# A fused cross-attention, attention and feed-forward layer: the engines' hand-written orders are rewritten

## What is computed

```python
x = x + matmul(fake_quant(layernorm(x)), fake_quant(ctx))   # ctx: [16, 1024, 1024], a matrix per sequence
q, k, v = split(layernorm(x) @ Wqkv)                        # 32 heads of 32, one k and one v head
probs = softmax(where(causal, q @ k.T * scale + alibi, -1e30))
x = x + (probs @ v) @ Wo
r = softmax(layernorm(x) @ gate_w.T)                        # 8 experts
x = x + (layernorm(x) * (r @ in_scale)) @ sign(weight).T * (r @ out_scale) + bias
```

## Time and profile before

| | |
|---|---|
| median of 3 runs | 466.38 us (464.2 to 466.59) |
| profiled execution, its own time | 469.97 us |
| its span in the profile | 468.1 us |
| busy: PE, DVE, ACT, POOL | 383.6, 314.0, 262.5, 127.6 us |
| moved by transfers | 91.96 MB |
| mean granted clock of TensorE | 0.905 |

### The profile page before, as it was taken

How to read it: one execution, slowest core, us unless ns; L and a number is a source line. 1 busy time by engine, 2 the same in 40 slices (tenths; PEclk the granted TensorE clock), 3 DMA queues, 4 the chain that set the end, 5 groups by cost and what they waited for, 6 DMA issues and landing times.

```text
span 468.1 us, 9132 instructions
## 1 busy us (share of the span) xinstructions
PE 383.6 (82%) x3712; PEld 253.2 (54%) x3712; DVE 314.0 (67%) x591; ACT 262.5 (56%) x309; POOL 127.6 (27%) x144
## 2 busy tenths in 40 slices
PE   0447825699795979989998999899989999989877
PEld 0116713594352577548754784478446945865354
DVE  7578576759747328874887489657975696486342
ACT  4787874565566855846484648473847372234021
POOL 4210041003610202603171317131623052116031
PEclk9956986599897979989998999899989999999958
DMA  8999985596748991659256846773675000100001
GB/s 322 378 410 409 406 326 179 191 406 208 254 148 295 260 355 46 228 224 282 99 194 259 209 145 214 270 213 126 225 270 158 3 1 1 47 1 1 0 22 70
DMA packets 30384, 91.96 MB, mean 196 GB/s; under 512 B 8256, under 2 KB 8512, under 8 KB 30336
## 3 DMA queue, kind: packets, MB, share of 16 engines
q1 hardware_dynamic: 28464, 84.45, 50.9%
q10 hardware_dynamic: 1872, 6.82, 4.2%
HBM read 85.50 MB, written 4.19 MB: 192 GB/s over the span
## 4 chain that ended last, share of the span: by engine, by line
PE 45%; DVE 24%; ACT 11%; DMA 6%; issue 6%; SPq 3%; POOL 3%; ACTq 0%; DVEq 0%
PE R L1558 9%; DMA ring<-ctx 6%; ACT b L573 6%; PE T L1386 4%; DVE st L926 3%; PE T L1509 3%; PE R L1422 3%; PE T L1467 3%; PE R L1425 3%; PE R L1424 3%; DVE XS_lo L876 3%; PE C L1367 3%; PE R L1338 2%; PE R L1339 2%; PE R L1340 2%
## 5 line engine op out<-in xcount | busy, mean ns | idle before, releaser
L573 ACT ACTIVATE b<-ring,quant,qpar 128x2048 uint8<-128x2048 f32 x64 | 132.5, 2091 | 15.0 <-DMA ring<-ctx 7.5
L1422 PE MATMUL R<-T_hi,Wqkv_hi 128*128 128x128 f16 x448 | 80.7, 224 | 0.0
L1424 PE MATMUL R<-T_lo,Wqkv_hi 128*128 128x128 f16 x448 | 80.5, 223 | 0.0
L1425 PE MATMUL R<-T_hi,Wqkv_lo 128*128 128x128 f16 x448 | 80.4, 223 | 0.0
L1367 PE MATMUL C<-b,aT 128*64 128x512 f16 x256 | 38.2, 435 | 21.6 <-ACT b L573 20.0
L329 POOL TENSOR_TENSOR Pr<-Pr,mx 128x512 f32<-128x512 f32 x16 | 18.9, 1182 | 132.6 <-DVE mx L1030 132.6
L1422 PEld LDWEIGHTS R<-T_hi,Wqkv_hi 128*128 128x128 f16 x448 | 45.5, 102 | 1.7
L1424 PEld LDWEIGHTS R<-T_lo,Wqkv_hi 128*128 128x128 f16 x448 | 44.9, 100 | 0.2
L1425 PEld LDWEIGHTS R<-T_hi,Wqkv_lo 128*128 128x128 f16 x448 | 44.9, 100 | 0.0
L1338 PE MATMUL R<-Wo,attT_hi 128*128 128x512 f16 x112 | 43.0, 384 | 0.5 <-DVE attT_lo L1048 0.5
L1339 PE MATMUL R<-Wo,attT_hi 128*128 128x512 f16 x112 | 43.0, 384 | 0.0
(11 more groups left out here) (167 smaller groups left out, 889.8 us busy)
## 6 DMA issues: line engine op xcount, KB each, us to landing
ring<-ctx SPq DMA_DIRECT2D x64, 1024.0 KB, 6.9
ring<-L_attn_Wo SPq DMA_DIRECT2D x4, 1024.0 KB, 5.2
ring<-L_ffn_weight SPq DMA_DIRECT2D x4, 1024.0 KB, 4.9
Wo<-L_attn_Wqkv SPq DMA_DIRECT2D x7, 544.0 KB, 15.3
X<-x ACTq DMA_DIRECT2D x7, 512.0 KB, 3.7
out<-X ACTq DMA_DIRECT2D x6, 512.0 KB, 7.2
sgn<-L_attn_Wqkv SPq DMA_DIRECT2D x1, 544.0 KB, 18.2
X<-x SPq DMA_DIRECT2D x1, 512.0 KB, 12.8
```

The costliest lines, as they stand in the source:

```text
L573: e.activation(b8[:, c % BRING, :], ring[:, slot, :], ACT.Identity, scale=qR2, bias=qZ2).then_inc(s_rf[slot], 1)
L1422: e.matmul(dst, hi, rows[0], start=k == 0 and g == 0, stop=False, skip_group_check=True)
L1424: e.matmul(dst, hi, rows[1], start=False, stop=False, skip_group_check=True)
L1425: last = e.matmul(dst, lo, rows[0], start=False, stop=k == KT - 1, skip_group_check=True)
```

## The change

It gives no engine a new instruction; it puts calls in another order, in four places.

- Steady openings (tiles 3 to 6): on VectorE norm0_rows of the next tile goes from before pt_lo(s, 1, ·) to behind result(s, 1), norm0_quant from the opening to the burst, behind norm2; GpSimd's with_row_sum follows it.
- Bursts: tk(s) goes before half of query(s, 0, low); k_lo before norm2; k_hi before conv(s.i + 1, 5); the row maximum of scores (0, 1) before xs.
- Tiles 0 and 1 (step_0, step_1): all four orders. conv(1, 5) to (1, 7) go before the exponentials that they followed; TensorE does t1, kv and half of query(1, 0) before pv(0), and pt(0, 1, ·) and pv(1) inside tile 1's queries; query(1, 0) no longer waits for V's parts; T's banks are handed out accordingly; GpSimd takes over VectorE's maximum subtractions of tiles 0 and 1.
- Burst 7 and tail: two of the feed-forward's k go before scores(7, 1), one behind the projections.

The diff, cut to its core:

```diff
@@ -93,8 +93,9 @@
 
-    uses = of(0, "T0") + of(1, "T0") + of(0, "T10 T11 Tk PT00 PT01 O0 PT10 PT11")
-    uses += of(1, "T10 T11") + of(0, "O1") + of(1, "Tk PT00 PT01 O0 PT10 PT11 O1")
+    uses = of(0, "T0") + of(1, "T0") + of(0, "T10 T11 Tk PT00 PT01") + of(1, "T10 T11")
+    uses += of(0, "O0") + of(1, "Tk") + of(0, "PT10 PT11 O1")
+    uses += of(1, "PT00 PT01 O0 PT10 PT11 O1")
     uses += of(0, "T20 T21 rl rT is0 is1")
@@ -485,26 +486,30 @@
                 inv_std(1, 0)
+                subtract_max(e, 0, 0, 0)
                 subtract_max(e, 0, 0, 1)
...
             def step_1(s, ahead):
+                subtract_max(e, 0, 1, 0)
                 normalize(0, 0, 0)
+                subtract_max(e, 0, 1, 1)
                 normalize(0, 0, 1)
-                subtract_max(e, 0, 1, 1)
+                inv_std(1, 1)
                 normalize(0, 1, 0)
                 normalize(0, 1, 1)
-                inv_std(1, 1)
-                inv_std(0, 2)
+                subtract_max(e, 1, 0, 0)
                 subtract_max(e, 1, 0, 1)
                 normalize(1, 0, 0)
+                subtract_max(e, 1, 1, 0)
+                subtract_max(e, 1, 1, 1)
                 normalize(1, 0, 1)
-                subtract_max(e, 1, 1, 1)
+                inv_std(0, 2)
                 normalize(1, 1, 0)
                 normalize(1, 1, 1)
+                with_row_sum(2)
+                inv_std(2, 0)
+                with_bias(0)
                 inv_std(0, 3)
-                inv_std(2, 0)
-                with_row_sum(2)
-                with_bias(0)
                 with_row_sum(3)
@@ -522,12 +527,12 @@
                 total(s.i - 2, 1)
-                if s.next:
-                    with_row_sum(s.i + 1)
 
...
                     inv_std(2, s.i - 1)
+                    if s.next:
+                        with_row_sum(s.i + 1)
                 subtract_max(e, s.i, 0, 1)
@@ -730,61 +735,61 @@
                 conv(1, 4)
+                conv(1, 5)
                 exp(0, 0, 0)
-                conv(1, 5)
-                exp(0, 0, 1)
 
...
                 conv(1, 6)
+                exp(0, 0, 1)
+                conv(1, 7)
+                pt_hi(s, 0, 0)
                 exp(0, 1, 0)
                 exp(0, 1, 1)
-                pt_hi(s, 0, 0)
                 pt_hi(s, 0, 1)
-                conv(1, 7)
-                o_hi(s, 0)
                 load_x(2)
                 load_x(3)
+                wo_hi(0)
+                wo_hi(1)
+                t1_hi(s, 0)
+                t1_hi(s, 1)
+                wo_hi(2)
+                k_copy(s)
+                v_copy(s)
+                wo_hi(3)
+                o_hi(s, 0)
+                k_hi(s)
+                q_hi(s, 0)
                 pt_hi(s, 1, 0)
                 pt_hi(s, 1, 1)
-                wo_hi(0)
-                t1_hi(s, 0)
-                t1_hi(s, 1)
+                sign(0)
                 o_hi(s, 1)
-                wo_hi(1)
-                k_copy(s)
-                v_copy(s)
-                wo_hi(2)
-                wo_hi(3)
-                k_hi(s)
-                sign(0)
-                q_hi(s, 0)
-                sign(1)
-                sign(2)
                 q_hi(s, 1)
                 exp(1, 0, 0)
-                sign(3)
                 exp(1, 0, 1)
-                conv(2, 0)
+                sign(1)
                 exp(1, 1, 0)
+                sign(2)
+                exp(1, 1, 1)
                 pt_hi(ahead, 0, 0)
                 pt_hi(ahead, 0, 1)
-                exp(1, 1, 1)
+                sign(3)
+                conv(2, 0)
+                o_hi(ahead, 0)
                 conv(2, 1)
-                o_hi(ahead, 0)
                 pt_hi(ahead, 1, 0)
...
                 conv(2, 2)
+                conv(2, 3)
                 o_hi(ahead, 1)
...
                 t2_copy(s, 1)
-                conv(2, 3)
+                conv(2, 4)
+                conv(2, 5)
                 router_exp(s)
-                conv(2, 4)
                 rt_copy(s)
-                conv(2, 5)
+                conv(2, 6)
                 xs_hi(s, 0)
                 xs_hi(s, 1)
-                conv(2, 6)
                 conv(2, 7)
@@ -941,7 +946,7 @@
 
-                at_least(e, s_T1, 2 * max(t - 1, 2) if t > 1 else 0)
+                at_least(e, s_T1, {0: 0, 1: 0, 2: 4, 3: 4}.get(t, 2 * t))
                 e.wait_ge(s_rstd[0], t + 1)
@@ -1145,7 +1150,8 @@
                 row_max(t, h, 0)
-                subtract_max(e, t, h, 0)
+                if t > 1:
+                    subtract_max(e, t, h, 0)
                 row_max(t, h, 1)
@@ -1171,42 +1177,37 @@
             def step_1(s, ahead):
-                scores_in(0, 1, 0)
+                softmax_in(0, 1)
                 row_sum(0, 0, 0)
-                scores_in(0, 1, 1)
-                row_max(0, 1, 0)
-                subtract_max(e, 0, 1, 0)
-                row_max(0, 1, 1)
                 row_sum(0, 0, 1)
-                row_sum(0, 1, 0)
+                x1(s)
                 pt_lo(s, 0, 0)
                 pt_lo(s, 0, 1)
+                norm1(s)
+                row_sum(0, 1, 0)
+                t1_lo(s, 0)
+                t1_lo(s, 1)
+                wo_lo(0)
                 row_sum(0, 1, 1)
-                x1(s)
+                v_lo(s)
+                wo_lo(1)
                 o_lo(s, 0)
-                norm1(s)
+                k_lo(s)
+                q_lo(s, 0)
                 pt_lo(s, 1, 0)
                 pt_lo(s, 1, 1)
-                wo_lo(0)
-                t1_lo(s, 0)
-                t1_lo(s, 1)
+                wo_lo(2)
+                softmax_in(1, 0)
                 o_lo(s, 1)
-                wo_lo(1)
-                v_lo(s)
-                wo_lo(2)
+                q_lo(s, 1)
                 wo_lo(3)
-                k_lo(s)
-                q_lo(s, 0)
+                row_sum(1, 0, 0)
+                softmax_in(1, 1)
+                row_sum(1, 0, 1)
                 stats0(2)
+                x2(s, 0)
                 norm0_rows(2)
                 norm0_quant(2)
-                q_lo(s, 1)
-                softmax_in(1, 0)
-                stats0(3)
-                row_sum(1, 0, 0)
-                row_sum(1, 0, 1)
-                softmax_in(1, 1)
-                x2(s, 0)
                 pt_lo(ahead, 0, 0)
@@ -1217,14 +1218,15 @@
                 o_lo(ahead, 1)
-                norm0_rows(3)
-                norm0_quant(3)
+                stats0(3)
                 router_max(s)
                 router_probs(s)
+                norm0_rows(3)
                 xs(s, 0)
...
                 xs_lo(s, 1)
+                norm0_quant(3)
                 x2(ahead, 0)
@@ -1245,23 +1247,24 @@
                     stats0(s.i + 1)
-                    norm0_rows(s.i + 1)
                 pt_lo(s, 1, 0)
...
                 o_lo(s, 1)
-                if s.next:
-                    norm0_quant(s.i + 1)
                 t1_lo(s, 0)
...
                 result(s, 1)
+                if s.next:
+                    norm0_rows(s.i + 1)
                 x2(s, 0)
...
                 v_lo(s)
+                k_lo(s)
                 norm2(s)
-                k_lo(s)
+                if s.next and not s.is_step(2):
+                    norm0_quant(s.i + 1)
                 q_lo(s, 0)
@@ -1269,9 +1272,9 @@
                 subtract_max(e, s.i, 0, 0)
+                row_max(s.i, 0, 1)
                 xs(s, 0)
                 xs(s, 1)
-                row_max(s.i, 0, 1)
                 xs_lo(s, 0)
@@ -1408,7 +1411,7 @@
                 if k_low(ks):
-                    if s.is_step(1):
+                    if s.is_step(1) and n == 1:
                         e.wait_ge(s_k, 2)
@@ -1550,7 +1553,7 @@
                 if n == 0 and s.i <= TILES:
-                    emptied(Step(s.i - 1), "is0" if k_low(ks) else "is1")
+                    emptied(Step(s.i - 1), "is0" if ks[0] < KT // 2 else "is1")
                 if s.i == TILES and n == 0:
@@ -1612,18 +1615,20 @@
                 pt(s, 0, 0)
+                context(1, 3)
                 pt(s, 0, 1)
-                context(1, 3)
+                t1(s)
+                kv(s)
+                query(s, 0, low[:2])
                 pv(s, 0)
+                query(s, 0, low[2:])
+                tk(s)
+                query(s, 0, high[:2])
                 pt(s, 1, 0)
                 pt(s, 1, 1)
-                t1(s)
+                query(s, 0, high[2:])
+                query(s, 1, low)
                 pv(s, 1)
-                kv(s)
-                query(s, 0, low)
-                tk(s)
-                query(s, 0, high)
-                query(s, 1, low)
                 scores(s, 0)
@@ -1698,10 +1704,12 @@
                     context(s.i + 1, 1)
+                else:
+                    ffn(Step(TILES), 0, low[:2])
                 scores(s, 1)
...
             def tail(s, last):
-                ffn(s, 0, low)
+                ffn(s, 0, low[2:])
                 pt(s, 0, 0)
```

(4 more changed lines are left out.)

## The result

The changed kernel takes 438.52 us (median of 4 runs, 437.58 to 439.17); the kernel before took 466.49 us beside it (4 runs, 464.2 to 470.46). The ratio is 0.939, with a 95% interval of 0.9323 to 0.9458: 28.0 us faster. The profiled execution took 438.96 us, of which 437.1 are the span.

The account below looks back on a forecast made before the run. TensorE, busy 383.6 of 468.1 us, was bounded by waits and half-clock stretches. 14.6 + 3.0 + 9.2 + 0.9 = 27.7 us off the profiled 469.97 gives 442.3; 3.6 lower for the median, 438.7, range 430 to 450.

Parts of the forecast that it names:

- The openings, 14.6 us: Openings of tiles 3 to 6: the wait for PT_lo and the half clock go, 3.64 us each, 14.6 in all.
- rival B: Openings: the wait goes but the half clock stays; they give 6.8 instead of 14.6, 446.5 us; chance 12%.
- The bursts, 0.6 us each: Bursts of tiles 2 to 6: waits for k_lo and qT_lo shrink or go, 0.6 us each, 3.0 in all.
- part 2: The bursts' term: norm2 behind k_lo makes t2 about 0.4 us late, net gain 0.2; qT_lo's wait of 0.44 goes.
- part 1: The openings' term: PT_lo runs directly after stats0; norm0_rows, 1.7 us, moves behind result(s, 1) and is just hidden.
- cover: VectorE's idle time before x2(s, 0) and x2(s, 1) in the openings, 1.75 us in all, claimed to hide the moved norm0_rows.
- Rival D: Bursts, tiles 4 to 7: aT comes late, so the kernel is slower; by bounds 470 us; chance 4%.
- The start, 9.2 us: Tiles 0 and 1: new orders gain 7.7, less 0.5 for tile 2's aT, plus 2.0 from conversion (2, 7).
- (c): Start: T_lo was ready 4.2 us after t1, behind a 2.29 us Wo low part that now follows; kv at 74.6.
- the walk: Start: following VectorE's order, with PT_lo of tile 1, to pv(ahead, 0) at 110 against 117.72, 7.7 us earlier.
- a to d: Start's landmarks: earlier conversions bring context(1, 3) 5.1 us earlier, t1 6.7 earlier, kv to 74.6, scores(1, 0) 10 earlier.
- The end, 0.9 us: Burst 7: feed-forward matmuls fill the wait before scores(7, 1) and qT_lo comes earlier; 0.9 us, between 0 and 2.

Follow-up runs that it names:

- experiment 8: The kernel before, unchanged, profiled once more: 466.34 us, span 464.5, with one fall of the clock in the openings instead of four.
- experiment 9: The changed kernel with norm2 again ahead of the low part of the keys (k_lo) in the bursts: 437.68 us.
- experiments 1: The kernel before with the openings' part of the change alone (norm0_rows behind result(s, 1), norm0_quant and with_row_sum in the burst): 456.76 us, ratio 0.9738.
- experiment 10: The changed kernel with tile 2's transpose into aT issued on SyncE ahead of the last two context loads: 436.53 us.
- Experiment 6: The kernel before with the new openings and new bursts together, start and last tile's tail as before: 447.25 us.
- experiments 4 and 5: First: changed kernel with conversions (1, 5) to (1, 7) back behind the exponentials, 443.49 us. Second: kernel before with only tile 1's conversions moved ahead, 464.35 us.

## Why the prediction was right, and where it was not

It said 438.7 us; the median is 438.52. The mechanism of each part is as put, but that it came within 0.2 us is luck. From profile to profile the gain was 31.0 us, 3.3 more than the 27.7 forecast, and the step from the profiled execution to the median was 0.4 us where 3.6 had been taken: two errors of some 3 us that cancel.

**The openings, 14.6 us.** Right for the profile on which it was worked out: length 24.04 us, clock 1.00, pv(s, 1) without idle time, rival B not seen in any opening of a kernel without the wait. (Tile 5's opening was 28.06 us, with a wait of 2.08, so the four terms come to 14.9.) But the term took 3.64 us in each of four openings as if the fall of the clock belonged to the program. Of it 1.7 is the wait, 0.2 the slower start of pv behind it, and 1.73 the fall, which an execution may have once (experiment 8) or four times, and of which 0.35 to 0.4 comes back in the burst.

**The bursts, 0.6 us each.** Measured: the steady period fell by 47.69 − 43.46 = 4.23 us, 3.64 in the opening and 0.59 in the burst. scores(s, 1) waits no more: GpSimd's subtraction ends at 213.25, XS_lo starts at 213.43 and takes 1.29 us. t2's wait for XL is 0.51 us, where part 2 had it "late by about 0.4" for k_lo alone. By the experiments k_lo's new place makes 0.2 of it (experiment 9; 0 to 0.17 with the bursts' changes alone) and the opening 0.3 (experiments 1 and 9): norm0_rows took 2.47 us beside GpSimd instead of the 1.7 of part 1, more than the 1.75 us of cover. Against the second profile of before, where the bursts' waits are 0.94 and 0.44, they gave 0.9. For norm0_quant the issue of aT was put at +6.4 us from the burst's beginning; it is at 203.64 − 197.17 = +6.5. The landing is not at +12.3 to +16.0 but at +9.5: the earlier trace rows held loads that were issued ahead, and in the new place there are none. Rival D was farther off than it seemed.

**The start, 9.2 us.** At context(2, 3) it is 9.03 us (147.22 to 138.19). The landmarks, predicted and measured: context(1, 3) 65.3, 65.55; t1 71.3, 72.53; kv 74.6, 75.96 (the terms that (c) gives, 71.3 + 4.2 − 2.29, make 73.2; what the rest is, it does not say); scores(1, 0) 90, 89.46; pv(ahead, 0) 110, 108.36; conversion (2, 7)'s 2.0 us, 1.92. Two errors inside it cancel: PT_lo came 1.6 us earlier than the walk said, and aT of tile 2, charged at 0.5 us, cost 1.90 (experiment 10). By the beginning of tile 3's opening the lead is 12.44 us, since this execution had 6.8 us of half clock between 138 and 159 where before's had 13.6 between 146 and 173. The 3.4 us beyond 9.03 are thus less half clock. Whether the order has a part in that is open: before tile 3's opening, from 134 us on, the profiles of kernels with the new start hold 3.4 to 13.7 us of half clock, those with the old one 6.8 to 13.7. Experiment 6 puts start and tail together at 8.7 us by the medians. That conversions and values belong together (a to d as one chain) is shown by experiments 4 and 5: 5.0 us by the medians (3.7 by the profile) if taken back, and 1.2 us at kv if added alone.

**The end, 0.9 us.** 1.25 in this profile; the wait before scores(7, 1) is 0.55 us instead of the 2.29 of the earlier trace rows.

**The step that was wrong is the last one:** "The same step puts the median at 438.7". The sum off the profile, 442.3, was 3.3 us too high (the profiled execution took 438.96), and the 3.6 us between before's profile and its median were carried over to the changed kernel, whose own profile lies only 0.4 us over its median. What the 3.6 us were is shown by experiment 8: three falls of the clock more in the openings, behind waits that the change removes. The right working would have taken the two apart: idle time from the rows, and each fall with the share of executions in which it comes.
